# A two-layer adaLN network on one core: load order, modulation rows, token splits and row updates of the first attention, and the order of the logits loop

## The reference, cut to what matters

```
mod_l = silu(c_l) @ wmod_l                      # (4, 6*256): SA CA GA SB CB GB, for each layer l
h     = layernorm(x) * (1 + CA) + SA            # first layer, per batch
q, k, v = split(h @ w_qkv.T)                    # _L0_attn_ref
agent = q @ w_conv1                             # (b, n)
attn  = softmax_c(sum_n agent * scale * k)      # (b, c)
score = softmax_n(v @ attn)                     # (b, n)
val   = sum_n score * v                         # (b, c)
x     = x + gate(GA) * (softmax(agent[..., None]) * val[:, None, :])
h     = layernorm(x) * (1 + CB) + SB            # input of the experts
logits = h @ Wr.T                               # (4096, 48); each expert takes its 128 best tokens
```

## Time and profile before

| | us |
|---|---|
| median of 3 runs (1788.21 to 1791.43) | 1790.55 |
| the profiled execution | 1788.67 |
| its span in the trace | 1786.9 |
| block `front`, 0 to | 113.17 |
| block "logits", from 113.17 to | 210.22 |

### The profile page before, as it was taken

How to read it: one execution, slowest core, us unless ns; L and a number is a source line. 1 busy time by engine, 2 the same in 40 slices (tenths; PEclk the granted TensorE clock), 3 DMA queues, 4 the chain that set the end, 5 groups by cost and what they waited for, 6 DMA issues and landing times. The chain is left out here.

```text
span 1786.9 us, 21261 instructions
## 1 busy us (share of the span) xinstructions
PE 1541.0 (86%) x7960; PEld 1270.6 (71%) x7960; DVE 1139.2 (64%) x1877; ACT 570.4 (32%) x817; POOL 311.6 (17%) x359
## 2 busy tenths in 40 slices
PE   7855343599999839999997899999995999999998
PEld 6532143599999836666663688888883888888887
DVE  5453499322222267778863887878774666698885
ACT  1013210133333212223222333333324544555452
POOL 2310000255555301221131500000000000000000
PEclk8766765699999969999998999999997999999999
DMA  5501491299999230121101300100004000000001
GB/s 188 213 1 48 133 332 66 59 295 293 296 297 291 45 118 24 36 67 40 36 24 47 106 16 22 35 24 24 12 12 156 25 23 13 1 1 24 19 17 36
DMA packets 127555, 157.06 MB, mean 88 GB/s; under 512 B 13937, under 2 KB 95977, under 8 KB 126449
## 3 DMA queue, kind: packets, MB, share of 16 engines
q1 hardware_dynamic: 115680, 138.12, 24.0%
q0 software_dynamic: 9216, 12.59, 3.4%
q10 hardware_dynamic: 2576, 5.26, 0.8%
HBM read 122.35 MB, written 33.60 MB: 87 GB/s over the span
## 5 line engine op out<-in xcount | busy, mean ns | idle before, releaser
L2227 PE MATMUL ff_down<-ff_w,ff_hid 128*128 128x256 f32 x1024 | 238.3, 379 | 0.0
L2227 PEld LDWEIGHTS ff_down<-ff_w,ff_hid 128*128 128x128 f32 x1024 | 193.4, 190 | 28.3
L1055 PE MATMUL h_ps<-xT,w 128*128 128x128 f32 x1536 | 194.0, 286 | 1.0 <-ACT xT L996 1.0
L1055 PEld LDWEIGHTS h_ps<-xT,w 128*128 128x128 f32 x1536 | 187.4, 199 | 1.6 <-issue 0.9
L1026 DVE TENSOR_TENSOR pre<-h_ps,b1T 128x1024 f32<-128x1024 f32 x48 | 58.8, 1224 | 177.4 <-PE h_ps L1055 177.4
L116 POOL TENSOR_TENSOR ff_rstd<-ff_var,minus_half 128x4 f32<-128x4 f32 x24 | 24.2, 1010 | 678.7 <-DVE ff_var L111 501.6
L2211 PE MATMUL ff_ring<-ff_rowsT_hi,ff_w_hi 128*128 128x512 f32 x256 | 121.3, 474 | 8.4 <-DVE ff_rowsT_lo L2005 5.6
L1090 PE MATMUL k_ring<-w_hi,hT_hi 128*128 128x512 f32 x256 | 118.5, 463 | 9.9 <-DVE hT_lo L1250 6.4
L1431 PE MATMUL k_acc<-wide_rows,hk 128*128 128x512 f32 x256 | 121.1, 605 | 4.4 <-ACT wide_rows L1375 4.4
L1090 PE MATMUL q_ring<-w_hi,hT_hi 128*128 128x512 f32 x256 | 109.7, 429 | 11.3 <-PEq L99 6.8
L1720 PE MATMUL q_out_ps<-kv_sums,wide_rows 128*128 128x256 f32 x512 | 115.6, 379 | 0.0
(11 more groups left out here) (360 smaller groups left out, 2979.1 us busy)
## 6 DMA issues: line engine op xcount, KB each, us to landing
w<-in_L_ffn_W_dram SPq DMA_DIRECT2D x48, 1024.0 KB, 5.8
w<-in_L_ffn_W_dram SPq DMA_DIRECT2D x48, 256.0 KB, 6.0
expert_sum_dram<-f_zero SPq DMA_DIRECT2D x8, 1024.0 KB, 14.4
b_rows<-in_L_ffn_b_dram SPq DMA_DIRECT2D x48, 128.0 KB, 8.4
x<-in_L_attn_x_dram SPq DMA_DIRECT2D x4, 1024.0 KB, 12.4
h_dram<-hg SPq DMA_DIRECT2D x8, 512.0 KB, 2.9
hk<-expert_sum_dram SPq DMA_DIRECT2D x8, 512.0 KB, 4.4
hT_hi<-expert_sum_dram SPq DMA_DIRECT2D x8, 512.0 KB, 5.3
```

Of the source, the lines that this page charges most:

```text
L1055: last = pe.matmul(h_ps[:, q % 2, s * KD + c, :], w1[:, q, s, k, c::KD], xT[:, q % 2, k, :], start=(k == 0), stop=(k == KD - 1))
L2227: last = pe.matmul(down[:, j // 2, j % 2, :], hid[:, n % 2, c, j * P:(j + 1) * P], w2[n // NG][:, c, :], start=(c == 0), stop=(c == CF - 1))
```

## The change

In `front`: SP loads only the first two sections of layer 0's `wmod` (0.5 MB) ahead of all of `x`, and the rest behind it. The transposed modulation is made in two parts: SA and CA at first (16 products), SB and CB in two later places of PE's list (8 each), with their copy on DVE near the end. DVE's statistics all come behind the probe. PE turns tiles 8 to 15 between the token products. Layer 0's modulation rows stay where they were; layer 1's three pieces go one by one behind `turn_mix`, the keys and the transposed `attn`. In the second token products PE has 12 tiles and DVE 20 (16 and 16 before). DVE gates batches 0 and 1 as soon as their values are there, and updates the rows of tiles 0 to 7 in this block.

In "logits": updates 0 and 1 are gone. ACT's order is normalise(n), rows(n-1), modulate(n). On PE the second half of group n-1's product comes behind the turn of group n. DVE copies the logits of n-2 where it copied those of n-1.

```diff
-PE_TILES = 2 * TB
+FIRST_TILES, SECOND_TILES, FRONT_UPDATES = 2 * TB, 3 * TB // 2, 2 * G
@@ SP
+                sp.dma_start(wmod[:, 0, :, 0:2 * D], weight[0][:, :, 0:2 * D]).then_inc(wmod_in[0], 16)
                 for b in range(B):
-                    if b == 2:
-                        sp.dma_start(wmod[:, 0], a["L0_wmod"].rearrange("(k p) n -> p k n", p=P)).then_inc(wmod_in[0], 16)
                     sp.dma_start(g.x[:, b * TB:(b + 1) * TB, :], source[b]).then_inc(x_in[b], 16)
-                sp.dma_start(wmod[:, 1], a["L1_wmod"].rearrange("(k p) n -> p k n", p=P)).then_inc(wmod_in[1], 16)
+                sp.dma_start(wmod[:, 0, :, 2 * D:], weight[0][:, :, 2 * D:]).then_inc(wmod_rest, 16)
+                sp.dma_start(wmod[:, 1], weight[1]).then_inc(wmod_in[1], 16)
@@ ACT: rows_of(0) where both layers were copied; rows_of(1) behind the exponential of the keys
@@ DVE
-                statistics(0)
-                statistics(1)
                 dve.wait_ge(modT_done, 1)
...
-                spread_probe()
-                statistics(2)
-                dve.wait_ge(wide_probe_done, 1)
-                row_dots(2)
-                statistics(3)
-                row_dots(3)
+                spread_probe(FIRST_TILES // TB)
+                for b in range(B):
+                    statistics(b)
+                    if b * TB >= FIRST_TILES:
+                        dve.wait_ge(wide_probe_done, 1)
+                        row_dots(range(b * TB, (b + 1) * TB))
...
-                spread_probe()
+                spread_probe(SECOND_TILES // TB)
                 dve.wait_ge(wide_probe_done, 2)
-                row_dots(2)
-                row_dots(3)
+                row_dots(range(SECOND_TILES, NT))
...
+                dve.wait_ge(modT_b_done, 1)
+                v(dve.tensor_copy(g.modT[:, 2:4].rearrange("p s k b -> p (s k b)"), ring[:, 0, 0:2 * KD * B]))
+                v(dve.tensor_scalar(g.modT[:, GAIN_B], g.modT[:, GAIN_B], 1.0, None, ALU.add))
+                dve.wait_ge(gate_in, 32)
+                dve.wait_ge(first_done, 1)
+                v(dve.tensor_tensor(g.gated[:, 0:2, :], wide[:, 0:2, :], mod[:, 0:2, GA, :], ALU.mult))
+                for j in range(FRONT_UPDATES):
+                    row = g.x[:, j, :]
+                    v.mark(dve.scalar_tensor_tensor(row, g.gated[:, j // TB, :], g.tok[:, j:j + 1], row, ALU.mult, ALU.add))
                 dve.wait_ge(value_done, 1)
-                dve.wait_ge(gate_in, 32)
-                v(dve.tensor_tensor(g.gated[:], wide[:], mod[:, :, GA, :], ALU.mult))
+                v.mark(dve.tensor_tensor(g.gated[:, 2:4, :], wide[:, 2:4, :], mod[:, 2:4, GA, :], ALU.mult))
+                v.sync()
@@ PE
+                modulation((SA, CA), MODT_A).then_inc(modT_done, 1)
                 turn_x(0)
                 turn_x(1)
-                turn_x(2)
                 pe.wait_ge(probed, 1)
                 sum_of(SUM, ...).then_inc(sum_done, 1)
                 pe.wait_ge(w_copied, 2)
-                wide_probe(1)
-                turn_x(3)
+                wide_probe(1, FIRST_TILES // TB)
+                for n in range(FIRST_TILES // G):
+                    if n >= 2:
+                        turn_x(n)
                     pe.wait_ge(xT_ready, KD * (n + 1))
+                    last = dots(DOT, range(n * G, (n + 1) * G))
...
-                for l in range(2):
-                    pe.wait_ge(wmod_in[l], 16)
-                    if l:
-                        pe.wait_ge(rows_copied, 1)
-                    for n in range(3):
-                        mod_rows(l, n)
+                pe.wait_ge(wmod_rest, 16)
+                for n in range(3):
+                    mod_rows(0, n)
...
                 turn_mix(1, MIX)
+                pe.wait_ge(wmod_in[1], 16)
+                pe.wait_ge(rows_copied, 1)
+                mod_rows(1, 0)
                 pe.wait_ge(mixT_ready, 1)
...              # keys
+                mod_rows(1, 1)
                 pe.wait_ge(attn_ready, 1)
...              # attn turned
+                mod_rows(1, 2)
                 pe.wait_ge(attnT_ready, 1)
...
-                wide_probe(2)
-                for n in range(PE_TILES // G):
-                    last = dots(DOT2, n)
-                last.then_inc(dots2_done, 1)
+                wide_probe(2, SECOND_TILES // TB)
+                dots(DOT2, range(SECOND_TILES)).then_inc(dots2_done, 1)
...
                 pe.matmul(PEAKS, ...).then_inc(peaks_done, 1)
+                pe.wait_ge(rows_copied, 2)
+                modulation((SB,), ring[:, 0, 0:KD * B])
...
                 turn_mix(2, MIX2)
+                modulation((CB,), ring[:, 0, KD * B:2 * KD * B]).then_inc(modT_b_done, 1)
@@ logits, DVE
-                        update(0)
                         statistics(0)
                         for n in range(NG):
-                            if n + 1 < NG:
+                            if FRONT_UPDATES // G <= n + 1 < NG:
                                 update(n + 1)
                             shift_of(n)
                             if n + 1 < NG:
                                 statistics(n + 1)
-                            if n:
-                                logits_copy(n - 1)
+                            if n >= 2:
+                                logits_copy(n - 2)
+                        logits_copy(NG - 2)
                         logits_copy(NG - 1)
@@ logits, ACT
-                        normalise(0)
                         for n in range(NG):
-                            if n + 1 < NG:
-                                normalise(n + 1)
+                            normalise(n)
                             if n:
                                 rows(n - 1)
                             modulate(n)
@@ logits, PE
+                        def half_logits(n, c):
+                            last = pe.matmul(lp[part(n), n % 2, :], wrT[:, c, :], hT[:, n % 2, c, :], start=(c == 0), stop=(c == KD - 1))
+                            if c == KD - 1:
+                                last.then_inc(logits_done, 1)
                         for n in range(NG):
...                          # z turned
+                            if n:
+                                half_logits(n - 1, 1)
                             pe.wait_ge(hT_ready, n + 1)
...                          # hT turned back
                             if n >= 2:
                                 pe.wait_ge(logits_out, n - 1)
-                            for c in range(KD):
-                                last = pe.matmul(...)
-                            last.then_inc(logits_done, 1)
+                            half_logits(n, 0)
+                        half_logits(NG - 1, 1)
```

More of the change, by code:

```diff
@@ L218, in _ @@
                     act.activation(wT[:, i], wide[:, 2 * i:2 * i + 2, :], ACT.Copy).then_inc(w_copied, 1)
-                for u in range(KD * PE_TILES // G):
+                for u in range(KD * FIRST_TILES // G):
                     n, k = u // KD, u % KD
@@ L281, in statistics, with row_dots @@
                     layer_norm_stats(v, g.spare, st, mv[:, tiles], var[:, tiles], TB, lambda j: g.x[:, b * TB + j, :], LN_EPS, var_ready)
-                def row_dots(b):
-                    for i in range(b * TB, (b + 1) * TB):
+                def row_dots(tiles):
+                    for i in tiles:
+                        b = i // TB
                         v.mark(dve.scalar_tensor_tensor(junk[:], g.x[:, i, :], 1.0, wide[:, b, :], ALU.mult, ALU.mult, accum_out=dot[:, i:i + 1]))
@@ L291, in row_sums @@
                     for j in range(TB):
-                        for b in range(PE_TILES // TB, B):
+                        for b in range(FIRST_TILES // TB, B):
                             i = b * TB + j
@@ L299, in row_sums, with spread_probe @@
                     dve.sem_inc(sums_x_ready, 1)
-                def spread_probe():
-                    for b in range(PE_TILES // TB, B):
+                def spread_probe(first):
+                    for b in range(first, B):
                         v.mark(dve.tensor_copy(spread[:, :, b, :], probe[:, :, b:b + 1].to_broadcast([P, KD, P])))
@@ L434, in turn_x, with dots @@
                         last.then_inc(x_turned, 1)
-                def dots(out, n):
-                    for i in range(n * G, (n + 1) * G):
+                def dots(out, tiles):
+                    for i in tiles:
                         for k in range(KD):
@@ L463, in turn_mix, with wide_probe @@
                     last.then_inc(mix_turned, 1)
-                def wide_probe(n):
+                def wide_probe(n, first):
                     pe.wait_ge(spread1_ready, n)
-                    for b in range(PE_TILES // TB, B):
+                    for b in range(first, B):
                         for k in range(KD):
@@ L471, in wide_probe, with modulation @@
                     last.then_inc(wide_probe_done, 1)
+                def modulation(sections, out):
```

(12 more changed lines are left out.)

38 lines of the change are left out of this document (18 added, 20 removed).

## The result

| | before | changed |
|---|---|---|
| median, us (runs) | 1790.59 (4) | 1726.70 (4: 1726.44, 1726.56, 1726.85, 1729.34) |
| ratio, 95% interval | | 0.9647 [0.9632, 0.9661] |
| the profiled execution / its span | 1788.67 / 1786.9 | 1729.34 / 1727.5 |
| block `front` | 113.17 | 100.50 |
| block "logits" | 97.05 | 49.04 |

The kernel is 63.9 us faster; 1729 was forecast. The two blocks give 12.67 + 48.01 = 60.7 us; the profiled spans differ by 59.4, since the blocks behind, which the change does not touch, scatter by some us. The profiled execution was the slowest of its four, so the medians differ by more.

A forecast was written before the change was run, and what follows sets the result against it. Latency, not a full engine, was taken as the bound: a ring in the logits block, a chain in the front. Front -12.9 and logits -47.3 sum to -60.2, from 1788.67 to 1728.5, a median of 1729; range 1722 to 1748.

The forecast's parts named there:

- load order and statistics: Front block, up to the first join: earlier modulation and moved statistics save 5.0 us, ends 2.5 and 5.3.
- rows out of the way: Front block: the weighted sum no longer stands behind layer 1's rows; saves 5.5 us, ends 2 and 6.9.
- second split: Second token products in the front block: 12 tiles on PE and 20 on DVE save 3.3 us.
- the rest of the front: Front block: late SB and CB products +0.2 us, gating of batches and updates +0.7; +0.9 in all.
- logits block: Logits block: DVE waits for an older copy, so the ring is cut; 49.7 us instead of 97.05, -47.3.
- PE is as late: Front block, first join: PE's turns, 64 dots and probe end at 36 to 39.7 us, beside DVE's 37.2.
- cold split: Second token products with PE at half clock: 13.55 us instead of 15.6 from wide probe to join, -2.0.
- warm one: Second token products with the clock up at the start: shorter probe, DVE's 9.7 us bounds; -4.1.
- The ring: Old logits loop: DVE's copy, update and shift, ACT and PE wait in turn, 11.64 us a trip without overlap.
- ACT's chain of 4.7: New logits loop at full clock: modulate, normalise, PE's turn, modulate again; 4.7 us per group.
- half clock in the loop: Rival, 17 in 100: PE stays at half clock in the logits loop, 7.3 us per group; total 1747.
- The slower rival: Rival, 2 in 100: the logits ring closes through the next group's turn, 17.4 us per group; +29, total 1818.

The follow-up runs named there:

- e1: The change's new front block with the old logits block of the kernel before; median 1771.85 us, ratio 0.9894.
- e8: The changed kernel with the third piece of layer 1's modulation rows moved behind the second token products; median 1728.92 us.
- e3: The changed kernel with both halves of a group's logits product together behind its turning back; median 1733.78 us.
- e4: The changed kernel with DVE copying the logits of n-1 again instead of n-2; median 1740.31 us.
- e5: The changed kernel with ACT's old order in the logits loop: normalise(n+1), rows(n-1), modulate(n); median 1734.78 us.
- e6: The changed kernel with each half logits product replaced by four 128-column transposes, so PE's loop has turns alone; median 1726.48 us, ratio 0.9641.
- e7: The changed kernel with the second token products split 16 and 16 tiles again; median 1730.40 us.
- e9: The changed kernel with layer 1's modulation rows made ahead of the first weighted sum again, in one piece; median 1733.02 us, ratio 0.9680.
- e12: The changed kernel itself run again, beside the kernel with all turns of x first and on the same chip; median 1726.65 us, ratio 0.9641.
- e2: The front block of the kernel before with the new logits loop, all eight updates in it; median 1744.30 us, ratio 0.9748.
- e11: The changed kernel with all four turns of x on PE ahead of the probe, not between the token products; median 1725.76 us, ratio 0.9653.

## Why the prediction was right

Each term beside what it measured, from the two profiled executions of the result:

| step | forecast | measured |
|---|---|---|
| load order and statistics, to the first join | -5.0 | -3.88 (42.12 to 38.24) |
| rows out of the way, to the second probe's sum | -5.5 | -5.74 |
| second split, to the second join | -3.3 | -3.90 (16.49 to 12.59) |
| the rest of the front | +0.9 | +0.85 |
| logits block | -47.3 | -48.0 |
| sum | -60.2 | -60.7 |

The sum fits better than its terms. The first join gave 1.1 us less than forecast and the second split 0.6 more, and the other six traces of the same front block end 0.1 to 3.1 us earlier, so the agreement of the front to 0.2 us is luck. The loop, 48 of the 61 us, is not: it came by its mechanism.

*First join.* Mis-sized by 1.1. "PE is as late" was right: PE, not DVE, ended it, and the modulation came at 13.19 for 13.4. But in this trace the whole 64 dots ran at half clock (6.83 + 3.57 + 3.57 = 13.97) and PE waited twice 0.69 for ACT's copies. So it was in e1 and e8 (6.83 again, joins at 38.27 and 38.17). In the seven other traces of this part (e3, e4, e5, e6, e7, e9 and e12) the first 32 dots took 3.7 to 5.1, and the join came at 36.5 to 37.1, the forecast's 37.2; DVE bounds it then.

*Rows.* Right in sum, and by its mechanism: e9 takes back 6.0 to 7.4 us up to the second probe's sum. The stretch from the join to the weighted sum fell by 6.38, and the pieces, 1.88 us each at the full clock, added 0.64 in the next one. Place by place they cost 0.12, nothing and 1.34 (forecast 0.4, nothing and 1.4), and the value probe, at the full clock now, gave 0.81 back (1.05 us instead of 1.87), which the forecast had named as possible.

*Second split.* The forecast mixed the split's own gain and that of the clock. It took -2.0 for a cold split, at half clock (e9: -2.56), and -4.1 for a warm one, at the full clock (-3.90; -2.58 in the three traces with the clock down at the wide probe). Of the 3.90, 2.25 stay with an even split (e7), so they are the clock's. The other 1.65 are not shown to be the split's, as e7's clock fell earlier. The forecast's guess that a PE busy with the pieces "may keep the full clock" was the decisive one. The value probe took 1.05 us in every trace with two or three pieces ahead of it and 1.87 in the three with none (before, e2, e9). For the 48 dots the pieces help in most traces, not in all (last section).

*Loop.* Right in place and size. The ring was read right, and in place of ACT's chain of 4.7 a trip of 4.65 was measured. The chain between ACT and PE, which the forecast did not price at the full clock, is as long, and by e6 ACT's own is 4.60. The rival "half clock in the loop", at 1747, fell with PEclk 1.00; e6 shows that it would have fallen without the wide products too, so the reason drawn from the earlier trace rows was the better of my two. What the prediction left out is that the longer copy distance alone does not open the ring: it names only the copy as the cut, and e5 shows that with ACT's old order the ring still closes, over two groups, at 5.5 us a group. The prediction had all three edits in its sum, so the time came out; the explanation was incomplete.

*The slower rival* (17.4 us a group) had the right question, whether the ring can close through the next group's turn. e4 is that ring: the copy that DVE waits for stands behind it, and the trip is 6.74, not 17.4. The copy's path has only the update, the shift, the normalisation, the turn and a half product in it, all at the full clock; the statistics, POOL's step, modulate, back and the row copy, which the 17.4 adds up, run beside it.

## What to carry to other kernels

When no engine is near full, write one trip of the loop down as a ring over the engines, with the group number at each step. A buffer's distance, the order on every engine and the length of a product each set how the ring closes; here any one of the three taken back cost 6 to 13 of the 48 us. Work moved off a critical path is best put where PE would be idle; its price there can be under its duration, as the pieces cost 0.64 us net for 3 x 1.88. And of a step made faster ahead of another engine's bound (e11) little is left: 0.9 of 3.5 us at the block's end. A term of 1 to 3 us in a block whose own traces differ by 3 can be read from neither two medians nor one trace: look first whether the clock was alike in both.

## What the runs showed of the hardware

*Narrow products let the clock fall though PE is never idle.* 48 products of one column behind 128-column loads were 100% busy at 0.50 in e8, and 64 of them before the change. Where the three 512-column pieces stood 4 to 11 us ahead of them, the 48 took 6.0 to 7.1 us in eight of nine traces, and 10.24 in the ninth (e11). With a piece fewer (e8) or none (e9) they took 10.24, one trace each. So the pieces help, but they are not enough, and not all that decides it is in the program: in e4, e5 and e6 the wide probe ran at half clock already, at the same distance from the pieces, and the clock rose again within the dots.

*The same program meets different clock states.* Seven traces with an identical front block ended it at 97.39, 97.49, 99.70, 99.84, 100.27, 100.41 and 100.50. They part in two places. The first 32 dots took 6.83 us in the traces that ended at 100.27 and 100.50, and 3.7 to 5.1 in the others. The second wide probe took 2.93 instead of 1.60 in those that ended at 99.70, 99.84 and 100.41. This is as large as the front edits that e7, e8 and e11 try. The clock column is no help at the start: it reads 1.00 for 19.17 to 26.00 in the changed kernel's trace, ahead of its first record, while 32 dots take 6.83 there, which is half clock.

*DVE steps with two SBUF operands and POOL held each other up.* In e11 four of the 14 row sums were long: 0.83, 0.71, 0.71 and 1.48 us, the other ten 0.47 to 0.49. Each of the four began 0.15 to 0.34 us behind the start of a POOL step (L267, L268, L270 and, for the longest, L272 at 45.80). The other traces have one long row sum (0.71 to 0.94) or none. The other way round, POOL's step in the logits loop took 2.95 us in e3 and 1.01 in the changed kernel:

```profile
123.94 2.95 POOL L116 TENSOR_TENSOR rstd<-var,minus_half 128x4 f32<-128x4 f32 x1 [2.55 <-DVE var L111]
```
```profile
124.83 1.01 POOL L116 TENSOR_TENSOR rstd<-var,minus_half 128x4 f32<-128x4 f32 x1 [3.64 <-DVE var L111]
```

In e3 DVE's four updates begin 0.43 us behind it, in the changed kernel 0.69. It was so for three steps of e3 and three of e6, where the next shift then waited 0.98 us for POOL. The Trainium skill ("SBUF — State Buffer", "SBUF: two separate sides") has an exclusive lock between the two in such a case, held for the whole instruction by the one that starts first. That each holds up the other agrees. That the first keeps it for its whole length is not what these records show: two row sums of 0.47 and 0.49 us run inside POOL's L268 of 2.11, and POOL's step, first by 0.43 us, is the one that waits. POOL's spans are rough in the profile, so this is a reading of ten records (four of DVE, six of POOL), not a rule.
